# Row maxima of the second and third pair of units as 64-row pairs, in slots 2 to 6 and 8 to 12

## The chip, the cores and the metric

One core of a Trainium2 chip. The metric is the time of one execution on the device in microseconds (us), median of the runs.

## The reference

A block of attention over images. x has 4 images of 256 channels and 32 x 32 = 1024 pixels. Cut to what matters:

```
x_n = group_norm(x, 32 groups) * gn_w + gn_b
q, k, v = 1x1 convolutions of x_n (256 x 256 weights and a bias each)
split into 4 heads of 64 channels
attn = softmax(q k^T / 8) over 1024 keys
out = x + 1x1 convolution of (attn v)
```

All is float32.

## The kernel before

**Units and slots.** An image has 8 units; a unit is one head and one half (512) of the queries. In order they are heads 0 and 1 of half 0, heads 0 and 1 of half 1, then heads 2 and 3 likewise. A unit takes 4 slots of 256 keys, so there are 32 slots to an image and 128 in all, G = 0 to 127. A pair V is units 2V and 2V+1: one half of the queries of two heads whose channels share one tile of 128 rows, 64 rows each.

**One slot.** TensorE (PE) forms the scores of 256 keys by 512 queries (`scores`, L711: four matmuls of 512 columns) in one of two double banks of PSUM: st[0] for even slots, st[1] for odd ones. ScalarE (ACT) takes the exponential twice (`exponent`, L909), once to 16 bits (p_hi) and once to 32 bits: into SBUF for odd slots (and slot 0), back into the scores' own bank for even ones. The difference, p_lo, is made by VectorE (DVE) for even slots, one slot later and in two halves (`p_low`, L1023), and by GpSimd (POOL) for the others. Four slots later PE weighs the values (`weigh`, L738: 24 narrow matmuls); after a unit's four slots DVE divides by the sums (`normalise`). Every second slot a job (a convolution of q, k, v or of the output) is begun on PE at its end and finished in the slot after, then evicted by ACT and split into high and low halves by POOL, whose tiles kq_hi and kq_lo hold one tile of 128 channels. SP copies these by DMA into k_both, k_one, q_twice and q_max, which the scores read.

**Maxima.** The softmax needs for each query a shift near its greatest score. PE forms the scores once more with the 16-bit values, 128 queries by 512 keys at a time, DVE reduces them (`row_max`, L995), after a unit's last one makes the shift (`row_shift`, L1010), and SP sends it by DMA as a row into q_max (`shift_to_row`, L490). The first scores of a unit wait for that (L719). A single maximum (L664, `single_maximum`) is one matmul on 128 rows (high and low keys) for one unit, in one of the two mx banks, and a reduction of 512. A pair (L679, `pair_of_maxima`) is two matmuls on 64 rows each, one per head, and a reduction of 2 x 512, in both mx banks or in the scores bank st[1]: there it waits for the odd slot's exponential (L690), and the next scores in st[1] wait until it is read (L728).

**Where they stand.** The order is written out by hand. Units 0 and 1 have singles straight from the tiles of k and q, begun ahead of slot 0 and ended in slot 1. Units 2 and 3 have singles from q_twice and k_both, two a slot: unit 2 in slots 2 to 5, unit 3 in slots 6 to 9. V = 2 (units 4 and 5) has pairs in slots 6, 8, 10, 10, 11, 12, 12, 13 (`FIRST_PAIRS`). V = 3 begins in slot 14, two to every even slot. In an even slot PE issues a pair's matmuls ahead of the weighing, in an odd listed slot behind it.

**Queues.** Each engine runs its own list in order. DVE's slot (in `slot` under `vector`): p_lo of the even slot before, then the maxima and a shift, the statistics of the next image, `normalise`, last single maximum of the slot; in slots 1 and 2 one half of channel_stats ends the slot. POOL's slot: cast and split of a job two slots back, p_lo, then the rest. The cast (`high`, L1219) waits until the tile's readers are done. SP first sends the shifts completed in the slot before, then its copies.

Of the kernel before, what the change touches and what calls it, by code (L numbers as in the profile page):

```python
# [12 lines left out]
def attention_block(nc, x, gn_w, gn_b, wq, bq, wk, bk, wv, bv, wp, bp, out):  # L13
# [9 lines left out]
    QT = HALF // P  # L23
# [6 lines left out]
    LAG = 4  # L30
    MX_AHEAD = 6
    MXJ = 2 * QT
    SINGLES = 4
    PAIR_AHEAD = 10
    PR = 8
    PB = 3
# [34 lines left out]
    FIRST_IMAGE = {0: ("q", 1, 0, 0), 2: ("v", 0, 1, 0), 4: ("k", 1, 1, 0), 6: ("q", 1, 1, 0), 8: ("v", 1, 0, 0)}  # L71

    MAX_MIDWAY = ((), (), ((0, 0), (0, 1)), ((0, 4), (0, 5)), (), ())
    FIRST_PAIRS = {6: (0,), 8: (1,), 10: (2, 3), 11: (4,), 12: (5, 6), 13: (7,)}
    FIRST_IN_SCORES = (0, 1, 2, 5)
    MAX_AFTER = ((), (), ((0, 2), (0, 3)), ((0, 6), (0, 7)), ((1, 0), (1, 1)), ((1, 2), (1, 3)))
    WARM = 4
    TAIL = 5
# [5 lines left out]
    with ctx:  # L84
# [153 lines left out]
        def wait(eng, s, v):  # L238
            if v > 0:
                eng.wait_ge(s, v)  # L240
# [41 lines left out]
        def pair_maxima(G):  # L282

            V, m = divmod(G + PAIR_AHEAD, 2 * SPU)
            if G in FIRST_PAIRS:
                return [("two", SINGLES // 2, m) for m in FIRST_PAIRS[G]]
            if V == LAST_PAIR:
                return [("two", V, m)]
            if m % 2 or not SINGLES // 2 < V < LAST_PAIR:
                return []  # L290
            return [("two", V, m), ("two", V, m + 1)]

        def in_scores_bank(V, m):

            return m in FIRST_IN_SCORES if V == SINGLES // 2 else V < LAST_PAIR and m % 2 == 0

        def maxima_at(G):
            return pair_maxima(G) + single_maxima(G)
# [12 lines left out]

        def one_slot_later(kind, n, m):

            return kind == "two" and SINGLES // 2 < n < LAST_PAIR and m % 2 == 1

        def reduced_at(G):

# [21 lines left out]

        def mx_part(U, j):  # L340

            return (j % QT, j // QT) if U < 2 else (j // 2, j % 2)

        def pair_part(m):
            return m % QT, m // QT

        def joined(U):

            return U + 1 if U < SINGLES else SINGLES + (U - SINGLES) // 2 + 1

        def units_joined(U):

# [13 lines left out]
        def tile_of(half, tile):  # L366

            return slice(half * HALF + tile, (half + 1) * HALF, QT)
# [9 lines left out]
        def unit(U):  # L378

            b, u = divmod(U, UNITS)  # L380
            return b, 2 * (u // 4) + u % 2, (u // 2) % 2
# [210 lines left out]
        def _(pe):  # L592
# [68 lines left out]
                                 start=False, stop=True, skip_group_check=True).then_inc(s_stat, 1)  # L661
                taken.append((s_gmean if kind == "mean" else s_gvar, b + 1))

            def single_maximum(U, j):  # L664
                if U < 2:
                    first_maximum(U, j)
                    return
                _, head, half = unit(U)
                if j == 0 and U == 2:
                    pe.wait_ge(s_first_top, 16 * 2)  # L670
                elif j == 0:
                    wait(pe, s_dup_k, 16 * 6)
                    wait(pe, s_dup_q[1], 16 * 6)
                wait(pe, s_mx_free, banks_read(("one", U, j)))
                tile, part = mx_part(U, j)
                nc.tensor.matmul(mxb[j % 2], q_twice[:, head, tile_of(half, tile)], k_both[:, head, halves(part)],
                                 start=True, stop=True).then_inc(s_mx_full, 1)

            def pair_of_maxima(V, m, G):  # L679

                b, head, half = unit(2 * V)
                tile, part = pair_part(m)
                if half == 0:
                    wait_hi(pe, "q", nth(head // 2, 0, b) + 1)
                    wait_hi(pe, "k", nth(head // 2, part, b) + 1)
                elif m == 0:
                    wait(pe, s_dup_k, 16 * 6 * (V // 2 + 1))
                    wait(pe, s_dup_q[1], 16 * 6 * (V // 2 + 1))
                if in_scores_bank(V, m):
                    wait(pe, s_exp, G)  # L690
                    bank = st[1]
                else:
                    wait(pe, s_mx_free, banks_read(("two", V, m)))
                    bank = mx
                for h in range(2):
                    rows = slice(h * D, (h + 1) * D)
                    if half == 0:
                        queries, keys = kq_hi["q"][rows, tile_of(0, tile)], kq_hi["k"][rows, halves(part)]
                    else:
                        queries = q_twice[rows, head + h, tile_of(1, tile)]  # L700
                        keys = k_both[rows, head + h, halves(part)]
                    last = nc.tensor.matmul(bank[:, h * HALF:(h + 1) * HALF], queries, keys, start=True, stop=True)  # L702
                last.then_inc(s_mx_full, 1)

            def maximum(item, G):
                if item[0] == "one":
                    single_maximum(*item[1:])
                else:
                    pair_of_maxima(*item[1:], G)

            def scores(G):  # L711
                U, s = divmod(G, SPU)
                _, head, half = unit(U)
                q = halves(half)
                if G == 1:
                    pe.wait_ge(s_e32["k"], 3)
                    pe.wait_ge(s_e32["q"], 2)
                if s == 0:
                    wait(pe, s_shift_dma[U % 2], 16 * (U // 2 + 1))  # L719
                if s == 0 and U < 2:  # L720
                    pe.wait_ge(s_first[U], 16 * 6)
                if s == 0 and U >= SINGLES and U % 4 == 0:
                    wait(pe, s_dup_k, 16 * 6 * (U // 4 + 1))
                    wait(pe, s_dup_q[0], 16 * 6 * (U // 4 + 1))
                if G > 1 and not in_place(G - 2):
                    wait(pe, s_exp, G - 1)
                if pair_in_bank(G) is not None:
                    wait(pe, s_mx_free, pair_in_bank(G) + 1)  # L728
                for c in range(CPS):
                    if G > 1 and in_place(G - 2):  # L730
                        wait_p_lo(pe, G - 2, c)
                    k = slice((CPS * s + c) * P, (CPS * s + c + 1) * P)
                    dst = st[G % 2][:, c * HALF:(c + 1) * HALF]
                    nc.tensor.matmul(dst, k_both[:, head, k], q_twice[:, head, q], start=True, stop=False)  # L734
                    last = nc.tensor.matmul(dst, k_one[:, head, k], q_max[:, head, q], start=False, stop=True)  # L735
                last.then_inc(s_st, 1)
# [464 lines left out]
        def _(pool):  # L1201
# [17 lines left out]
            def high(kind, i, j, b):  # L1219
                wait(pool, s_e32[kind], nth(i, j, b) + 1)  # L1220
                wait(pool, s_dup_k if kind == "k" else s_dup_q[j], 16 * 6 * (2 * b + i))
                if (i, b) == (1, 0):
                    wait(pool, s_mx_full, 2 * MXJ)
                elif (i, b) > (0, 0):
                    gone = 2 * (2 * b + i - 1)
                    if kind == "k":
                        wait(pool, s_mx_full, place_of["two", gone, (j + 1) * QT - 1] + 1)
                    elif j == 0:
                        wait(pool, s_mx_full, all_full("two", gone))
                nc.gpsimd.tensor_copy(kq_hi[kind][:, halves(j)], e32[kind][:, j, :]).then_inc(s_hi[kind], 1)  # L1230
# [40 lines left out]
            def slot(G):  # L1271
                b, g = place(G)
                todo = job_at(G - 2) if G % 2 == 0 else None
                if todo and todo[0] in "kq":
                    high(*todo)
                    low_kq(pool, *todo)
                if todo and todo[0] == "v":
                    split_values(*todo[1:])
                if slot_of(G - 1) is not None and not lo_on_dve(G - 1):
                    p_low(G - 1)  # L1280
                if G == 1:
                    high("k", 1, 0, 0)
                    low_kq(pool, "k", 1, 0, 0)
                if todo and todo[0] == "y":
                    residual(*todo[1:])
                if output_at(G):
                    split_output(*output_at(G))
                stat = stat_at(G)
                if G % 2 and job_at(G - 1) and job_at(G - 1)[0] not in LONG:
                    stat = job_at(G - 1)  # L1290
                if stat and stat[0] == "mean":
                    about_group_mean(pool, stat[-1])
                if stat and stat[0] == "var":
                    norm_factors(stat[-1])
                lows = FIRST_Z_LOW if b == 0 else Z_LOW
                if b + 1 < B and g in lows:
                    z_low(pool, b + 1, lows.index(g))
                if b == B - 1 and g in (21, 23):
                    add_bias((g - 21) // 2)
# [52 lines left out]
```

## Time and profile before

| | us |
|---|---|
| median of 3 runs | 366.53 (366.32 to 366.99) |
| the profiled execution | 366.61 |
| its span | 364.9 |
| PE busy | 348.4 (95%) |
| ACT busy | 302.1 (83%) |
| POOL busy | 284.2 (78%) |
| DVE busy | 283.2 (78%) |

TensorE's granted clock is full in all 40 slices of the span. Matmuls overlap: the time of one in a row is from its start to its modelled end, and what it takes of PE is the distance between two starts. PEld is the load of weights, SPq the queue of SP's DMA issues.

### The profile page before, as it was taken

To read this page: it belongs to the slowest core of one execution; us is meant where nothing else is said; L and a number is where in the kernel's file an instruction comes from. 1 tells how busy PE (TensorE), PEld (TensorE's weight loads), DVE (VectorE), ACT (ScalarE), POOL (GpSimd) and SP (SyncE) were. 2 spreads that over 40 slices of the span, in tenths; PEclk is the share of its full clock that TensorE was granted. 3 is DMA by queue.
4 is the path that set the end of the run, shared out by engine and by line. 5 is a ranking of instruction groups with operands and counts; after the bars stand their busy time and mean duration, and the time that the engine had idled before them with its cause. 6 is when DMAs were issued, how large, how long until landed. Compare 5 with 4: busy or idle time off the path is not lost.

```text
span 364.9 us, 11249 instructions
## 1 busy us (share of the span) xinstructions
PE 348.4 (95%) x4581; PEld 209.4 (57%) x4581; DVE 283.2 (78%) x445; ACT 302.1 (83%) x361; POOL 284.2 (78%) x258
## 2 busy tenths in 40 slices
PE   0999999999999999999999999999999999999996
PEld 0634564655656565655666556565656556655564
DVE  4889899878888687878887777777877787787474
ACT  1748879998887999989877999988889888888982
POOL 5064989699778998988778998988979797967722
PEclk9999999999999999999999999999999999999999
DMA  6046241123743440261643342031552451060113
GB/s 206 25 131 160 45 97 38 31 91 85 135 129 74 93 98 31 29 184 38 131 146 66 72 88 70 8 82 43 117 164 50 96 91 60 2 203 2 31 31 118
DMA packets 38731, 30.92 MB, mean 85 GB/s; under 512 B 23820, under 2 KB 31512, under 8 KB 38680
## 3 DMA queue, kind: packets, MB, share of 16 engines
q1 hardware_dynamic: 37936, 29.15, 32.8%
q10 hardware_dynamic: 744, 1.06, 0.8%
q8 instruction: 37, 0.61, 0.7%
q14 instruction: 14, 0.11, 0.1%
HBM read 9.44 MB, written 4.19 MB: 37 GB/s over the span
## 4 chain that ended last, share of the span: by engine, by line
PE 84%; DVE 9%; ACT 2%; issue 2%; DMA 1%; DVEq 1%; POOL 0%; ACTq 0%
PE gen L612 19%; PE st L734 13%; PE st L735 13%; PE pv L757 9%; PE pv L760 8%; PE pv L759 7%; PE st L702 5%; PE mx L702 3%; DVE mx L1003 3%; PE st L612 2%; DVE p_lo L1029 2%; PE mx L815 1%; ACT st L924 1%; DVE mx L999 1%; DMA xin<-in_x_dram 1%
## 5 line engine op out<-in xcount | busy, mean ns | idle before, releaser
L919 ACT ACTIVATE p_hi<-st 128x1024 f16<-128x1024 f32 x127 | 130.7, 1029 | 41.2 <-PE st L735 40.6
L1268 POOL TENSOR_TENSOR p_lo<-p,p_hi 128x1024 f16<-128x1024 f32 x62 | 132.2, 2132 | 10.2 <-ACT p L924 10.2
L757 PEld LDWEIGHTS pv<-v_hi,p_hi 128*128 128x128 f16 x1024 | 93.4, 97 | 26.7 <-issue 14.7
L757 PE MATMUL pv<-v_hi,p_hi 128*128 128x65 f16 x1024 | 106.5, 195 | 0.3 <-DVE o L1037 0.2
L759 PE MATMUL pv<-v_lo,p_hi 128*128 128x64 f16 x1024 | 106.0, 193 | 0.0
L760 PE MATMUL pv<-v_hi,p_lo 128*128 128x65 f16 x1024 | 105.8, 194 | 0.0
L1029 DVE TENSOR_TENSOR p_lo<-st,p_hi 128x512 f16<-128x512 f32 x126 | 80.9, 684 | 31.6 <-ACT st L924 31.3
L734 PE MATMUL st<-q_twice,k_both 128*128 128x512 f16 x256 | 97.1, 379 | 1.6 <-DVE p_lo L1029 1.2
L759 PEld LDWEIGHTS pv<-v_lo,p_hi 128*128 128x128 f16 x1024 | 93.9, 99 | 6.2
L735 PE MATMUL st<-q_max,k_one 65*128 65x512 f16 x256 | 97.3, 380 | 0.0
L760 PEld LDWEIGHTS pv<-v_hi,p_lo 128*128 128x128 f16 x1024 | 93.9, 97 | 0.0
L1003 DVE TENSOR_REDUCE mx<-st 128x2 f32<-128x1024 f32 x52 | 63.7, 1226 | 24.2 <-PE st L702 24.0
L1003 DVE TENSOR_REDUCE mx<-mx 128x2 f32<-128x1024 f32 x60 | 73.1, 1218 | 1.6 <-PE mx L702 1.6
L924 ACT ACTIVATE st<-st 128x1024 f32<-128x1024 f32 x63 | 65.6, 1041 | 0.0
L924 ACT ACTIVATE p<-st 128x1024 f32<-128x1024 f32 x64 | 65.2, 1018 | 0.0
L734 PEld LDWEIGHTS st<-q_twice,k_both 128*128 128x128 f16 x256 | 25.4, 99 | 26.3 <-issue 6.9
L735 PEld LDWEIGHTS st<-q_max,k_one 65*128 65x128 f16 x256 | 25.0, 98 | 18.4
L453 POOL TENSOR_TENSOR st_lo_k<-e_k,st_hi_k 128x512 f16<-128x512 f32 x16 | 18.5, 1157 | 9.6 <-ACT e_k L894 7.6
L1247 POOL TENSOR_TENSOR y<-y,xres 128x512 f32<-128x512 f32 x14 | 17.7, 1269 | 7.6 <-ACT y L903 7.6
L999 DVE TENSOR_REDUCE mx<-mx 128x1 f32<-128x512 f32 x32 | 20.9, 685 | 2.9 <-PE mx L815 1.4
L612 PE MATMUL gen<-w_hi_v,z_hi 128*128 128x128 f16 x128 | 23.1, 219 | 0.0
L612 PE MATMUL gen<-w_hi_v,z_lo 128*128 128x128 f16 x128 | 23.0, 219 | 0.0
(183 smaller groups left out, 545.0 us busy)
## 6 DMA issues: line engine op xcount, KB each, us to landing
q_twice<-st_hi_q SPq DMA_DIRECT2D x64, 64.0 KB, 2.1
xres<-in_x_dram SPq DMA_DIRECT2D x4, 1024.0 KB, 5.2
out_dram<-y SPq DMA_DIRECT2D x13, 256.0 KB, 2.3
xin<-in_x_dram SPq DMA_DIRECT2D x6, 512.0 KB, 4.7
k_both<-st_hi_k SPq DMA_DIRECT2D x16, 128.0 KB, 2.3
k_one<-st_hi_k SPq DMA_DIRECT2D x16, 128.0 KB, 2.6
q_max<-st_lo_q SPq DMA_DIRECT2D x32, 64.0 KB, 2.1
k_both<-st_lo_k SPq DMA_DIRECT2D x16, 128.0 KB, 2.3
```

The lines of the kernel that those rows point to most:

```text
L612: last = nc.tensor.matmul(dst, a, c, start=first and t == 0 and n == 0, stop=t == CT - 1 and n == 2, skip_group_check=True)
L702: last = nc.tensor.matmul(bank[:, h * HALF:(h + 1) * HALF], queries, keys, start=True, stop=True)
L734: nc.tensor.matmul(dst, k_both[:, head, k], q_twice[:, head, q], start=True, stop=False)
L735: last = nc.tensor.matmul(dst, k_one[:, head, k], q_max[:, head, q], start=False, stop=True)
L757: nc.tensor.matmul(pv_v[:, q, :], hi, vh, start=k == 0 and q == 0, stop=False, skip_group_check=True)
L759: nc.tensor.matmul(pv_v[:, q, 0:D], hi, vl, start=False, stop=False, skip_group_check=True)
L760: last = nc.tensor.matmul(pv_v[:, q, :], lo, vh, start=False, stop=k == NK - 1, skip_group_check=True)
L919: nc.scalar.activation(p_hi[:, G % PR, :, :], scores, ACT.Exp, scale=SM_SCALE / M_SCALE)
L924: nc.scalar.activation(p_full(G), scores, ACT.Exp, scale=SM_SCALE / M_SCALE).then_inc(s_exp, 1)
L1003: last = nc.vector.reduce_max(mx8[:, n % 2, :, tile, part], bank[:, :].rearrange("p (h k) -> p h k", h=2), AX.X)
L1029: nc.vector.tensor_tensor(p_lo[:, G % PR, c, :], p_full(G)[:, c, :], p_hi[:, G % PR, c, :], ALU.subtract).then_inc(s_plo_dve, 1)
L1268: nc.gpsimd.tensor_tensor(p_lo[:, G % PR, :, :], p_full(G), p_hi[:, G % PR, :, :], ALU.subtract)\
```

## The change

Units 2 and 3 lose their singles. They become the pairs of V = 1, straight from the tiles of k and q, in slots 2 to 6 (two pairs in even slots, one in odd ones). The pairs of V = 2 go to slots 8 to 12 in the same pattern. In each, pairs 0, 3 and 6 use the scores bank. Both shifts of units 2 and 3 are now made in slot 6. Since V = 1 reads the tile of k, POOL's cast of the second tile of k over its first half goes from slot 1 to slot 5 and waits for pairs of V = 1; the casts after it wait likewise. The first scores of unit 2 get a wait for the copies of q.

```
-    SINGLES = 4
+    SINGLES = 2
+    BY_LIST = 2
...
-    FIRST_PAIRS = {6: (0,), 8: (1,), 10: (2, 3), 11: (4,), 12: (5, 6), 13: (7,)}
-    FIRST_IN_SCORES = (0, 1, 2, 5)
+    FIRST_PAIRS = {2: ((1, 0), (1, 1)), 3: ((1, 2),), 4: ((1, 3), (1, 4)), 5: ((1, 5),), 6: ((1, 6), (1, 7)),
+                   8: ((2, 0), (2, 1)), 9: ((2, 2),), 10: ((2, 3), (2, 4)), 11: ((2, 5),), 12: ((2, 6), (2, 7))}
+    FIRST_IN_SCORES = {1: (0, 3, 6), 2: (0, 3, 6)}
...
             if G in FIRST_PAIRS:
-                return [("two", SINGLES // 2, m) for m in FIRST_PAIRS[G]]
+                return [("two", *pair) for pair in FIRST_PAIRS[G]]
...
-            return m in FIRST_IN_SCORES if V == SINGLES // 2 else V < LAST_PAIR and m % 2 == 0
+            return m in FIRST_IN_SCORES[V] if V <= BY_LIST else V < LAST_PAIR and m % 2 == 0
...
-            return kind == "two" and SINGLES // 2 < n < LAST_PAIR and m % 2 == 1
+            return kind == "two" and BY_LIST < n < LAST_PAIR and m % 2 == 1
...
             def pair_of_maxima(V, m, G):
...
-                if half == 0:
-                    wait_hi(pe, "q", nth(head // 2, 0, b) + 1)
+                if half == 0 or V == 1:
+                    wait_hi(pe, "q", nth(head // 2, half, b) + 1)
...
-                    if half == 0:
-                        queries, keys = kq_hi["q"][rows, tile_of(0, tile)], kq_hi["k"][rows, halves(part)]
+                    if half == 0 or V == 1:
+                        queries, keys = kq_hi["q"][rows, tile_of(half, tile)], kq_hi["k"][rows, halves(part)]
...
             def scores(G):
...
+                if s == 0 and U == 2:
+                    wait(pe, s_dup_q[1], 16 * 6)
...
             def high(kind, i, j, b):
...
                 if (i, b) == (1, 0):
-                    wait(pool, s_mx_full, 2 * MXJ)
+                    if kind == "k":
+                        wait(pool, s_mx_full, place_of["two", 1, (j + 1) * QT - 1] + 1)
+                    else:
+                        wait(pool, s_mx_full, 2 * MXJ if j == 0 else all_full("two", 1))
...
-                if G == 1:
+                if G == 5:
                     high("k", 1, 0, 0)
                     low_kq(pool, "k", 1, 0, 0)
```

`single_maximum` and `joined` are removed, being without a caller.

## Rows read from the trace of the kernel before

**Rows 1.** The page: busy time by engine, and the chain's shares.
```profile
PE 348.4 (95%) x4581; PEld 209.4 (57%) x4581; DVE 283.2 (78%) x445; ACT 302.1 (83%) x361; POOL 284.2 (78%) x258
...
PE 84%; DVE 9%; ACT 2%; issue 2%; DMA 1%; DVEq 1%; POOL 0%; ACTq 0%
```

**Rows 2.** Stages: edges, length, then busy us of PE, PEld, DVE, ACT, POOL; clock; DMA.
```profile
32.27:37.09 4.82, 4.32 (x37) 2.51 (x37) 4.42 (x10) 4.50 (x6) 2.49 (x4) 1.00 0.39 83
37.09:49.06 11.97, 11.96 (x138) 6.87 (x139) 10.21 (x20) 8.92 (x11) 11.32 (x12) 1.00 0.28 61
49.06:70.99 21.93, 20.75 (x296) 13.11 (x295) 20.22 (x30) 19.85 (x25) 17.90 (x21) 1.00 0.24 51
```

**Rows 3.** Timeline of PE, slots 3 to 6: start, duration, operation, [idle before].
```profile
34.52 0.38 PE L734 MATMUL st<-q_twice,k_both 128*128 128x512 f16 x1
...
37.09 0.38 PE L734 MATMUL st<-q_twice,k_both 128*128 128x512 f16 x1 [0.44 <-DVE p_lo L1029]
...
37.60 0.39 PE L734 MATMUL st<-q_twice,k_both 128*128 128x512 f16 x1
...
40.25 0.38 PE L734 MATMUL st<-q_twice,k_both 128*128 128x512 f16 x1
...
42.92 0.38 PE L734 MATMUL st<-q_twice,k_both 128*128 128x512 f16 x1
...
43.58 0.38 PE L735 MATMUL st<-q_max,k_one 65*128 65x512 f16 x1
43.89 0.41 PE L702 MATMUL st<-st_hi_k,st_hi_q 64*128 64x512 f16 x2
44.23 0.41 PE L676 MATMUL mx<-k_both,q_twice 128*128 128x512 f16 x1
```

**Rows 4.** Timeline of DVE, slots 2 to 6.
```profile
34.22 1.29 DVE L999 TENSOR_REDUCE mx<-mx 128x1 f32<-128x512 f32 x2
35.43 0.68 DVE L1058 BATCH_NORM_STATS2 bn<-xin 128x6 f32<-128x512 f32 x1
...
36.31 1.24 DVE L1029 TENSOR_TENSOR p_lo<-st,p_hi 128x512 f16<-128x512 f32 x2
37.46 1.88 DVE L999 TENSOR_REDUCE mx<-mx 128x1 f32<-128x512 f32 x3
...
44.34 1.23 DVE L1003 TENSOR_REDUCE mx<-st 128x2 f32<-128x1024 f32 x1
45.48 0.68 DVE L999 TENSOR_REDUCE mx<-mx 128x1 f32<-128x512 f32 x1
```

**Rows 5.** Timeline of SP's DMA issues: the shift of unit 1.
```profile
34.78 0.51 SPq L494 DMA_DIRECT2D q_max<-shift  x1
```

**Rows 6.** Timeline of PE's weight loads, the first of slot 4.
```profile
37.06 0.10 PEld L734 LDWEIGHTS st<-q_twice,k_both 128*128 128x128 f16 x1 [0.73 <-DMA q_max<-shift]
```

**Rows 7.** The tile shift, whole kernel: its 32 DMAs.
```profile
DMA to landing us min/median/max: 1.9/2.0/3.5
```

**Rows 8.** Timeline of ACT, the two exponentials of slot 5.
```profile
41.32 1.02 ACT L919 ACTIVATE p_hi<-st 128x1024 f16<-128x1024 f32 x1 [1.13 <-PE st L735]
42.24 1.02 ACT L924 ACTIVATE p<-st 128x1024 f32<-128x1024 f32 x1
```

**Rows 9.** Timeline of PE, slot 16: weighing begins behind two pairs.
```profile
72.51 0.20 PE L757 MATMUL pv<-v_hi,p_hi 128*128 128x65 f16 x1
```

**Rows 10.** Timeline of DVE, slot 13: last maximum of V = 2 and its shift.
```profile
65.10 1.23 DVE L1003 TENSOR_REDUCE mx<-mx 128x2 f32<-128x1024 f32 x1
...
66.75 0.17 DVE L1020 TENSOR_SCALAR shift<-mx 128x8 f16<-128x8 f32 x1
```

**Rows 11.** Timeline of POOL: casts of k in slots 1 and 6, z_b.
```profile
34.69 0.61 POOL L1230 CAST st_hi_k<-e_k 128x512 f16<-128x512 f32 x1 [2.19 <-SPq L578]
...
45.17 0.61 POOL L1230 CAST st_hi_k<-e_k 128x512 f16<-128x512 f32 x1
...
52.40 0.20 POOL L1217 TENSOR_TENSOR z_b<-beta_z,z_m 128x2 f32<-128x2 f32 x1
```

More of the change, by code:

```diff
@@ L285, in pair_maxima @@
             if G in FIRST_PAIRS:
-                return [("two", SINGLES // 2, m) for m in FIRST_PAIRS[G]]
+                return [("two", *pair) for pair in FIRST_PAIRS[G]]
             if V == LAST_PAIR:
                 return [("two", V, m)]
-            if m % 2 or not SINGLES // 2 < V < LAST_PAIR:
+            if m % 2 or not BY_LIST < V < LAST_PAIR:
                 return []
@@ L340, in mx_part @@
         def mx_part(U, j):
-            return (j % QT, j // QT) if U < 2 else (j // 2, j % 2)
+            return j % QT, j // QT
         def pair_part(m):
             return m % QT, m // QT
-        def joined(U):
-            return U + 1 if U < SINGLES else SINGLES + (U - SINGLES) // 2 + 1
         def units_joined(U):
@@ L662, in statistic @@
                 taken.append((s_gmean if kind == "mean" else s_gvar, b + 1))
[L664 to L677, printed above, removed]
             def pair_of_maxima(V, m, G):
@@ L706, in maximum @@
                 if item[0] == "one":
-                    single_maximum(*item[1:])
+                    first_maximum(*item[1:])
                 else:
```

## The prediction

> **What bounds the kernel now.** The page first: PE is busy 95% of the span and holds 84% of the chain that ended last, VectorE (DVE) 9% [rows 1]. So time is gained or lost where PE stands still or gets fewer passes. The change touches slots 1 to 13 only, so the stage table comes next. Its edges are starts of scores: of slot 2 (32.27), 4 (37.09), 8 (49.06) and 16 (70.99). In slots 2 and 3 PE is busy 4.32 of 4.82 us, and DVE, at 4.42, more than PE. In slots 4 to 7 PE is full, 11.96 of 11.97. In slots 8 to 15 it idles 1.18 of 21.93, with DVE busy 20.22 [rows 2]. Two engines are near full at once: work moved forward in DVE's order can stop PE even if there is less of it.
>
> The timeline then shows the links. Scores of an even slot wait for p_lo of the slot two before, which DVE makes in two halves: DVE begins it at 36.31, PE begins the halves of slot 4 at 37.09 and 37.60, so 0.78 and 1.29 later [rows 3, 4]. Those scores also stood behind the DMA of the shift row: issued 34.78, PE's weight load released at 37.06, 2.28 us [rows 5, 6]; over the kernel such DMAs land in 1.9 to 3.5 us [rows 7]. Of the exponential: scores begin at 40.25, ScalarE (ACT) at 41.32 (1.07 later), and its second pass ends at 42.24+1.02 = 43.26, 1.94 after its start [rows 3, 8].
>
> **Prices.** A 512-column pass is 0.22 us of PE: three spacings from 42.92 to 43.58; scores are four, 0.87. A pair between full-height work: scores of slot 6 end at 42.92+0.87 = 43.79, the next operation starts at 44.23, so 0.44 though both halves run at once [rows 3]. Two pairs in a row: 70.99+0.87 = 71.86 to weighing at 72.51, 0.65 [rows 2, 9]. On DVE two single maxima take 34.22 to 35.43 (1.21 to the next operation). One pair's starts 0.45 after its matmuls (43.89, 44.34) and takes 1.23, 1.14 until the next operation (45.48) [rows 3, 4]. The two halves of p_lo take 1.15 to 1.20 (36.31 to 37.46 here; 1.20 is taken). From a unit's last pair maximum to its shift: 65.10+1.23 = 66.33 to 66.75+0.17 = 66.92, 0.59 [rows 10].
>
> Here row and rule can be weighed. By the rows a lone pair (0.44) costs what two singles cost (2 x 0.22); only the second of two pairs is cheap (0.21). The Trainium skill, TensorEngine Tiling (Array Packing), Theoretical Speedup, promises up to 2x at 64 rows or fewer, by which 16 passes would become 8 and PE would save 1.74 us; its Key Properties say that a change of tiling mode drains TensorE, and the trace's 0.44 agrees with that. The sum goes by the rows.
>
> **Step 1, slots 2 to 4: +1.07.** DVE reaches the first maximum of slot 2 at 34.22, behind the shift of unit 1 and channel_stats, as now [rows 4]. There stand two singles (1.21); the change puts two pairs there (2.28), both ahead of the other half of channel_stats and p_lo of slot 2. p_lo goes from 36.31 to 37.38. Two things follow. The first pair is in the scores bank, so scores of slot 3, now at 34.52, wait until it is read: 34.22+1.23 = 35.45, about +1.0. Scores of slot 4 wait for p_lo: 38.16 and 38.67 for 37.09 and 37.60, +1.07.
>
> **Step 2, slot 4: +0.52.** Scores end at 39.1, the first pair runs to 39.44, and the second needs the maxima bank: DVE starts slot 3's pair only after p_lo, 37.38+1.20 = 38.58, and ends at 39.81. Second pair from 39.9 to 40.24. What is left of the 2.65 from the late half to the next scores (37.60 to 40.25) without that half (0.44), two singles (0.44) and some 0.16 of waiting is 1.6 for weighing, statistic and job: next scores at about 41.84, against 40.25, +1.59 in all. All of PE's queue stands behind this wait: the weighing, the mean's matmul, the job whose tile POOL splits. Low end +0.07 (the wait hidden), high +0.6.
>
> **Step 3, slots 5 to 7: -0.42.** Slot 5 swaps two singles for a lone pair (0.43, 0.44): nothing. Slot 6 saves 0.22 of passes, but its second pair waits for slot 5's, issued last thing in that slot: nothing again. Slot 7 loses two singles, -0.43; PE could begin scores of slot 8 at 49.06+1.07+0.52-0.42 = 50.23.
>
> **Step 4, slot 8: +0.97.** The lead shrinks: unit 2's shift, now made in slot 5, comes with unit 3's at the end of slot 6. Scores of slot 6 start at 42.92+1.59 = 44.51; slot 5's pair just before at 44.17, reduced to 45.85; the two of slot 6 follow on DVE from 45.93: 1.14+1.23 = 48.30, shift 48.89, DMA issued at 48.92, landed 2.28 later: 51.20. PE waits 0.97. With the landing at 1.9 or 3.5 us it is 0.59 or 2.19. Queued behind: slot 8's scores, both pairs, a weighing and the job. The wait added there for q's copies costs nothing: SP issues them ahead of unit 1's shift (34.78), so they land some 13 us earlier.
>
> **Step 5, slots 8 to 15: -0.65.** Before: five lots of pairs (three lone, two double) and four singles: 3x0.44+2x0.65+4x0.22 = 3.50; after, three doubles and two lone: 2.83. DVE has 4 x 0.60 less and the same pairs, but these stand closer: in slots 10 to 14 three doubles, the p_lo passes, normalise and the shift follow one another. I take PE's saving alone; bounds 0 (DVE keeps the pace) and -1.2 (all 1.18 of idle time goes too). Unit 4's shift comes one slot sooner, and does not bound now.
>
> **Moved on other queues: 0.** On POOL the cast of k (0.61) and its split leave slot 1, where it idled 2.19 us behind SP's count, for slot 5 [rows 11]. q's then stands first at the same count, and the time saved is handed back in slot 5. There the wait on the fourth pair (PE at 39.2) is over; slot 6's cast of k, now at 45.17, waits for the eighth (46.4), with a split, p_lo and the norm factors behind it. z_b, now ready at 52.60, moves as far, to 53.8; ACT asks for it after slot 8's exponential, at 51.20+1.07+1.94 = 54.2. If that cover goes, the excess falls on ACT. SP issues the same shift DMAs, two together instead of one and one; its copies of k wait for that split and are not read before slot 16. From slot 16 the order is the old one and PE the limit, so the lag stays.
>
> **The sum.** +1.07+0.52-0.42+0.97-0.65 = +1.49. The profiled execution took 366.61 us (span 364.9 and 1.7 around it), so 368.1 on its own time; it lies 0.08 above the median 366.53, so **368.0** on the median. Bounds: all low ends 1.07+0.07-0.42+0.59-1.20 = +0.1; all high ends 1.07+0.6-0.42+2.19+0 = +3.4.
>
> **Rivals.** *PE's passes decide, faster.* If DVE's early maxima were off the path, only the passes would count: slots 2 to 7 hold twelve singles and a lone pair, 3.08, and get 2.83: -0.25; with step 5 -0.9, so 365.6. For: PE full in slots 4 to 7. Against: DVE busier than PE in slots 2 and 3. It decides if slot 3's scores start by about 34.7. By the page's 2x this rival would come to 364.8. Chance 0.14.
> *Caught up, no change.* The lag arises but slots 8 to 15 give it back, DVE being freed of 2.4 us of singles and PE having 1.18 of idle there: 1.49-1.2+0.65 less a prompt landing (0.38) is +0.6, and with step 2's wait hidden +0.1: 366.6. For: DVE's 20.22 of 21.93. Against: the pairs crowd in slots 8 to 12. 0.16.
> *The shift lands late.* At 3.5 us, behind other copies, step 4 is 2.19: +2.7, 369.2. For: the largest landing in the view; against: nothing else is issued just ahead. 0.12.
> That the pairs don't run at once is excluded by the row at 43.89.
>
> **How the numbers follow.** Forecast 0.58, so slower (by over 0.2%, 0.73 us, about what a measurement of this kernel can tell from no change) 0.58+0.12 = 0.70; same 0.16; faster 0.14. The range leaves out the faster case and the tail of the late landing: 366.4 to 369.3. The forecast's own range is 367.3 to 368.8.
>
> **What would show it.** Right: slot 3's scores wait for a DVE maximum until about 35.5; slot 4's start near 38.2; PE stands before slot 8's scores for the shift's DMA, about 1 us; from slot 16 on scores stand 1.5 us later than before, constant to the end. Wrong: scores of slot 8 by 49.5, or a lag that shrinks to nothing by slot 16.

## The result, and the profile after

The changed kernel takes 369.14 us (median; 368.69 to 370.04) against 366.76 for the kernel before: ratio 1.0067, 95% interval 1.0053 to 1.0081, so 2.4 us slower. The forecast was slower by 1.5 (368.0), the range 366.4 to 369.3. The profiled execution took 370.04 us (span 368.3), the longest of its four.

The page after, its lines of busy time and of the chain's shares, to set beside [rows 1]:

```profile
PE 348.7 (95%) x4581; PEld 209.6 (57%) x4581; DVE 282.4 (77%) x435; ACT 302.4 (82%) x361; POOL 284.0 (77%) x258
...
PE 83%; DVE 8%; ACT 3%; issue 2%; DVEq 2%; DMA 2%; ACTq 0%
```

No engine works more than 0.3 us longer; the other 3 of the 3.4 us that the span grew are waiting. The stages, as in [rows 2], at the starts of scores of slots 2, 4, 8 and 16:

```profile
34.04:39.94 5.90, 4.62 (x40) 2.47 (x40) 5.50 (x10) 4.53 (x6) 4.21 (x4) 1.00 0.40 90
39.94:52.53 12.59, 11.80 (x138) 6.52 (x138) 10.61 (x17) 9.08 (x11) 10.11 (x12) 1.00 0.06 11
52.53:73.82 21.29, 20.15 (x293) 12.59 (x293) 17.39 (x23) 19.79 (x25) 17.55 (x20) 1.00 0.33 71
```

The lengths were 4.82, 11.97 and 21.93: slots 2 and 3 gained 1.08, slots 4 to 7 gained 0.62, slots 8 to 15 lost 0.64. That is 1.06 in all, and the same steps can be followed slot by slot. Below, a lag is the start of a slot's first exponential less that of slot 2, minus the same difference in the trace of the kernel before. ACT's rows for slots 2 and 16, before:

```profile
33.35 1.02 ACT L919 ACTIVATE p_hi<-st 128x1024 f16<-128x1024 f32 x1
...
72.61 1.04 ACT L919 ACTIVATE p_hi<-st 128x1024 f16<-128x1024 f32 x1
```

and after, where the difference is 40.32 instead of 39.26:

```profile
35.13 1.03 ACT L904 ACTIVATE p_hi<-st 128x1024 f16<-128x1024 f32 x1
...
75.45 1.04 ACT L904 ACTIVATE p_hi<-st 128x1024 f16<-128x1024 f32 x1
```

From there the lag is constant: 1.06 at slot 16, 1.11 at slot 126. Two more parts lie outside the changed slots. Slot 2's exponential is already 1.78 later than before, and from slot 126's exponential (352.72 before, 355.61 after) to the end of the span it takes 12.69 us instead of 12.18. The sum is 1.78+1.11+0.51 = 3.40.

DVE in slots 2 to 4 after, to set beside [rows 4]:

```profile
36.00 1.23 DVE L988 TENSOR_REDUCE mx<-st 128x2 f32<-128x1024 f32 x1
37.14 1.22 DVE L988 TENSOR_REDUCE mx<-mx 128x2 f32<-128x1024 f32 x1
38.27 0.68 DVE L1043 BATCH_NORM_STATS2 bn<-xin 128x6 f32<-128x512 f32 x1
39.02 0.21 DVE L1045 BATCH_NORM_AGGREGATE mv<-bn 128x2 f32<-128x12 f32 x1
39.15 1.23 DVE L1014 TENSOR_TENSOR p_lo<-st,p_hi 128x512 f16<-128x512 f32 x2
40.30 1.22 DVE L988 TENSOR_REDUCE mx<-mx 128x2 f32<-128x1024 f32 x1
```

and PE's rows that waited for it, then the first scores of slot 8 (beside [rows 3]):

```profile
37.37 0.38 PE L719 MATMUL st<-q_twice,k_both 128*128 128x512 f16 x1 [0.71 <-DVE mx L988]
...
39.94 0.38 PE L719 MATMUL st<-q_twice,k_both 128*128 128x512 f16 x1 [0.52 <-DVE p_lo L1014]
...
41.66 0.41 PE L685 MATMUL mx<-st_hi_k,st_hi_q 64*128 64x512 f16 x2 [0.27 <-DVE mx L988]
...
52.53 0.39 PE L719 MATMUL st<-q_twice,k_both 128*128 128x512 f16 x1 [0.42 <-DMA q_max<-shift]
```

Each predicted wait is there: slot 3's scores for the first pair, slot 4's for p_lo, the second pair of slot 4 for the bank, slot 8's for the shift. The last is shorter than reckoned: SP issued that DMA at 50.59 and PE went on 1.94 us later, not 2.28.

```profile
50.59 1.15 SPq L492 DMA_DIRECT2D q_max<-shift  x2
```

What was not predicted stands ahead of slot 2. PE's eight warming passes take 1.91 us, the first pass of the first job 0.63 instead of 0.39 (the granted clock reads 1.00 in this stretch in both traces), and the first scores wait 1.13 us for the first shift row, whose DMA landed in 3.5 us instead of 1.9:

```profile
13.08 1.91 PE L814 MATMUL st<-group_avg,ident 128*128 128x128 f32 x8
14.78 0.63 PE L610 MATMUL st<-z_hi,w_hi_q 128*128 128x512 f16 x1
...
29.19 0.38 PE L719 MATMUL st<-q_twice,k_both 128*128 128x512 f16 x1 [1.13 <-issue]
```

The same passes in the trace of before:

```profile
13.16 1.12 PE L829 MATMUL st<-group_avg,ident 128*128 128x128 f32 x8
14.38 0.39 PE L612 MATMUL st<-z_hi,w_hi_q 128*128 128x512 f16 x1
```

### The profile page after: what moved, and what is told of

It reads as the page before. It is cut to its first block, busy times and chain, and to the rows that moved or that the text cites. A ratio compares the mean times of both kernels' runs of the same rounds, so it can differ in the third digit from the quotient of the medians.

```text
span 368.3 us, 11245 instructions
## 1 busy us (share of the span) xinstructions
PE 348.7 (95%) x4581; PEld 209.6 (57%) x4581; DVE 282.4 (77%) x435; ACT 302.4 (82%) x361; POOL 284.0 (77%) x258
## 3 DMA queue, kind: packets, MB, share of 16 engines
q10 hardware_dynamic: 744, 1.06, 0.8%
HBM read 9.44 MB, written 4.19 MB: 37 GB/s over the span
## 4 chain that ended last, share of the span: by engine, by line
PE 83%; DVE 8%; ACT 3%; issue 2%; DVEq 2%; DMA 2%; ACTq 0%
PE gen L610 19%; PE st L719 13%; PE st L720 13%; PE pv L742 9%; PE pv L745 7%; PE pv L744 7%; PE st L685 5%; PE mx L685 4%; DVE mx L988 4%; DVE p_lo L1014 2%; PE st L610 2%; DVEq L978 2%; ACT st L909 1%; PE mx L800 1%; DMA xin<-in_x_dram 1%
## 5 line engine op out<-in xcount | busy, mean ns | idle before, releaser
L988 DVE TENSOR_REDUCE mx<-st 128x2 f32<-128x1024 f32 x54 | 66.2, 1226 | 26.5 <-PE st L685 26.3
L988 DVE TENSOR_REDUCE mx<-mx 128x2 f32<-128x1024 f32 x66 | 80.4, 1218 | 3.8 <-PE mx L685 3.8
L610 PE MATMUL gen<-w_lo_v,z_hi 128*128 128x128 f16 x128 | 23.0, 219 | 0.0
```

The lines of the kernel that those rows point to most:

```text
L610: last = nc.tensor.matmul(dst, a, c, start=first and t == 0 and n == 0, stop=t == CT - 1 and n == 2, skip_group_check=True)
L988: last = nc.vector.reduce_max(mx8[:, n % 2, :, tile, part], bank[:, :].rearrange("p (h k) -> p h k", h=2), AX.X)
```

## The experiments

Theory: the slots lose 1.06 us by DVE's order and the shift's lead, the rest is start and end. Rivals: PE's passes or the exponentials hold the slots, or the start belongs to the changed program. The lags, with ratios to the kernel before measured beside each run:

| run | lag at slot 3 | 5 | 8 | 16 | ratio (interval) |
|---|---|---|---|---|---|
| changed kernel | 1.07 | 1.58 | 1.70 | 1.06 | 1.0067 (1.0053 to 1.0081) |
| changed, again | 1.07 | 1.58 | 1.70 | 1.06 | 1.0050 (1.0031 to 1.0069) |
| statistics later | 1.07 | 0.76 | 0.88 | 0.23 | 1.0036 (1.0016 to 1.0056) |
| earlier seventh pair | 1.07 | 1.58 | 1.58 | 0.77 | 1.0019 (1.0000 to 1.0038) |
| 16 memsets | 1.07 | 1.58 | 1.70 | 1.05 | 1.0035 (1.0020 to 1.0049) |
| V = 2 spread | 1.07 | 1.58 | 1.70 | 1.32 | 1.0055 (1.0042 to 1.0068) |
| later half and seventh pair | 1.07 | 0.77 | 1.52 | 0.72 | 1.0037 (1.0023 to 1.0051) |
| both halves and seventh pair | 0.57 | 0.27 | 1.02 | 0.21 | 1.0035 (1.0020 to 1.0051) |
| both halves, memsets | 0.58 | 0.28 | 0.39 | -0.25 | 0.9990 (0.9975 to 1.0006) |
| the same, odd pairs ahead | 0.58 | 0.28 | 0.57 | -0.13 | 0.9993 (0.9980 to 1.0006) |

**Both kernels again**, without an edit. The kernel before:

> The kernel before, unchanged, once more. In the changed kernel's trace the first exponential starts at 30.26 us against 28.36, ahead of every slot that the change touches: 0.7 us of TensorE at a lower granted clock and a first shift row that landed in 3.5 us instead of 1.9. Theory A (chance of the execution): the start varies from run to run, so this trace may show the first exponential anywhere from 28.4 to 30.3, and the ratio is 1.000 within 0.002. Theory B (the changed program's own start): here the first exponential stays near 28.4 and the shift lands in about 2 us.

The lower granted clock of which this expectation speaks does not stand ahead of slot 2 in the changed kernel's trace: it reads 1.00 in every stretch up to 367 us, and 0.50 only in the last 1.3 us, when PE has no work left.

Ratio 0.9996 (0.9979 to 1.0013). Its profiled execution was a long one (369.58): the first shift landed in 3.4 us, the first exponential started at 29.64, and a granted clock of 0.51, near the lower of its two levels, between 30.3 and 33.7 us (0.78 over 28 to 32) took slot 2 to 36.07. So a late first landing and a disturbed start belong to the execution. The lags stay: -0.11 at slot 8 and -0.12 at slot 16.

> The changed kernel, unchanged, once more. Theory A: the first exponential comes back towards 28.4 us and the time towards the kernel before plus the slots' own 1.1 us, a ratio of about 1.003. Theory B: the first shift row lands in 3.5 us again, the first exponential starts near 29.5, and the ratio stays at 1.006 to 1.007. Both: from slot 2 to slot 15 the exponentials fall back by 1.06 us against the kernel before.

The lags are those of the first trace. The landing was 1.9 us here, yet the ratio is 1.0050 and the first exponential started at 29.07, 0.71 late: neither theory holds whole. Of the 2.3 us that its span (367.2) is longer, 0.71 lie ahead of slot 2, 1.02 are the lag at slot 126 and 0.57 come behind it.

**The second half of the statistics later:**

```diff
-                if G in (1, 2):
-                    channel_stats(1, 1, (G - 1,))
+                if G in (1, 3):
+                    channel_stats(1, 1, (G // 2,))
```

> The changed kernel with the second half of channel_stats moved from the end of DVE's slot 2 to the end of its slot 3, so that p_lo of slot 2 follows the two pairs directly. My theory of step 1 (DVE's work ahead of p_lo holds PE): scores of slot 4 start 0.6 us sooner after those of slot 2 and those of slot 5 0.85 sooner than in the changed kernel, and the whole is 0.8 us faster than it. Rival (the exponential or the passes of PE hold slots 3 and 4): no change against the changed kernel.

Lag at slot 5 0.76 instead of 1.58, at slot 16 0.23 instead of 1.06: 0.83 gained, against 0.8 expected. DVE's rows of slots 2 and 3 show p_lo directly behind the pairs:

```profile
34.62 1.23 DVE L988 TENSOR_REDUCE mx<-st 128x2 f32<-128x1024 f32 x1
35.77 1.22 DVE L988 TENSOR_REDUCE mx<-mx 128x2 f32<-128x1024 f32 x1
36.90 1.28 DVE L1014 TENSOR_TENSOR p_lo<-st,p_hi 128x512 f16<-128x512 f32 x2
38.09 1.22 DVE L988 TENSOR_REDUCE mx<-mx 128x2 f32<-128x1024 f32 x1
39.23 0.68 DVE L1043 BATCH_NORM_STATS2 bn<-xin 128x6 f32<-128x512 f32 x1
```

Scores of slot 4 start 0.60 us sooner after those of slot 2, and those of slot 5 0.82 sooner. No pass of PE and no exponential changed, so from slot 4 on it is DVE's order that holds PE, and the rival falls. Slot 3's lag is still 1.07: this edit leaves what stands ahead of the first pair as it was. In times the gain does not stand clear: the median is 368.43 against 368.96 for the changed kernel beside it, and the two ratios' intervals overlap.

**The seventh pair of V = 1 in slot 5:**

```diff
-... 5: ((1, 5),), 6: ((1, 6), (1, 7)),
+... 5: ((1, 5), (1, 6)), 6: ((1, 7),),
-    FIRST_IN_SCORES = {1: (0, 3, 6), 2: (0, 3, 6)}
+    FIRST_IN_SCORES = {1: (0, 3, 7), 2: (0, 3, 6)}
         def ahead_of_weighing(G):
...
+            if G == 5:
+                return 1
```

> The changed kernel with the seventh pair of V = 1 moved from slot 6 to slot 5 (the sixth ahead of the job and the weighing there, the seventh behind them), so that slot 6 has one pair and the shift is ready about 0.45 us sooner after the first scores of slot 5 and PE's wait for its DMA before slot 8 (0.42 us in the changed kernel's trace) is gone. My theory of step 4: slot 8's scores start 0.4 us sooner against those of slot 2 than in the changed kernel, the whole 0.4 us faster than it. Rival (the passes alone count): within 0.1 us of it.

The wait for the DMA ahead of slot 8 is gone, but slot 5 is 0.45 longer (lag at slot 6 2.05 instead of 1.60), so slot 8's lag fell by 0.12 only, not 0.4; at slot 16 by 0.29. The last pair, now in the scores bank, also made slot 7's scores wait 0.21 for the shift itself. The direction was right, the gain smaller.

**Sixteen memsets.** DVE lost ten instructions by the change. The DMA view of the changed kernel's trace between 365.4 and 366.4 us, 2.75 us ahead of the end, has

```profile
q14 instruction: 1, 0.01, 4.6%
```

In the first trace of the kernel before the last packet of that queue is 7.25 us ahead of the end. (A packet of the other instruction queue, q8, is 4.5 us ahead of the end there, and 7.0 in the changed kernel.) The four last DVE operations of the changed kernel take

```profile
363.81 1.56 DVE L1055 SCALAR_TENSOR_TENSOR y<-st,xres 128x256 f32<-128x256 f32 x4 [0.68 <-PE st L610]
```

where they take 1.42 before. That is 0.14 of the 0.51 us; the other 0.38 lie between the last of them and the end (2.93 us against 2.55), where only output DMAs are left. The edit:

```diff
+        spare = sb("spare", [P, 16])
...
+                if 36 <= G < 52:
+                    nc.vector.memset(spare[:, G - 36:G - 35], 0.0)
```

> The changed kernel plus 16 one-element memsets on DVE into a tile that nothing reads, one in each of slots 36 to 51. The four traces of changed programs have a packet of the instruction queue 14 about 2.8 us ahead of the end, the two of the kernel before at 7.3; from the 127th exponential to the end of the span they take 12.7 to 13.0 us against 12.2 and 12.5. Theory (fewer DVE instructions move a fetch of code into the last output): here the packet is no longer in the last 4 us, that stretch takes 12.2 to 12.5 and the kernel is 0.4 us faster than the changed one, with the same lag of 1.06 us from slot 2 to 15. Rival (the stretch is long for another reason): 12.7 and the same time.

Nothing useful was added, and the end came back: the packet is 8.25 us ahead, the stretch behind slot 126's exponential 12.20 us, the four operations

```profile
362.97 1.42 DVE L1056 SCALAR_TENSOR_TENSOR y<-st,xres 128x256 f32<-128x256 f32 x4 [0.69 <-PE st L611]
```

The lag did not move. The ratio is 1.0035 here, 1.0050 and 1.0067 without, and the intervals of the first two overlap; its own trace had a late first landing (3.5 us) again. Over all traces the stretch is 12.16 to 12.20 us in the three programs with the memsets, 12.69 to 12.97 in the seven traces without, and 12.11 to 12.49 in four of the kernel before. So the packet's place moves with the number of DVE instructions (435, 445 and 451), and the longer end goes with it. That this packet itself holds up the last output is argued, not shown.

**V = 2 spread:**

```diff
-... 8: ((2, 0), (2, 1)), 9: ((2, 2),), 10: ((2, 3), (2, 4)), 11: ((2, 5),), 12: ((2, 6), (2, 7))}
+... 8: ((2, 0),), 9: ((2, 1),), 10: ((2, 2), (2, 3)), 11: ((2, 4),), 12: ((2, 5), (2, 6)), 13: ((2, 7),)}
-    FIRST_IN_SCORES = {1: (0, 3, 6), 2: (0, 3, 6)}
+    FIRST_IN_SCORES = {1: (0, 3, 6), 2: (0, 2, 5)}
```

> The changed kernel with the pairs of V = 2 over slots 8 to 13 in the numbers 1, 1, 2, 1, 2, 1, as the kernel before has them over 6 to 13, instead of 2, 1, 2, 1, 2. Step 5 by PE's passes: two doubles and four lone pairs in place of three and two cost 0.23 us, so the lag at slot 16 is 1.3 instead of 1.06. Rival (DVE's crowd in slots 10 to 14 bounds): the lag at slot 16 is 0.8 or less.

1.32 at slot 16, from 1.06, as expected, but not for the reason expected. From one slot's first scores to the next, slot 8 is 0.15 us shorter here than in the changed kernel (one pair instead of two), slot 13 is 0.20 shorter although it has a pair more, and slot 14 is 0.62 longer. There the second pair of V = 3 waits for the maxima bank, since the last maximum of V = 2 is made in slot 13 again and its shift comes that much later. The kernel before has the same row,

```profile
66.98 0.41 PE L702 MATMUL mx<-k_both,q_twice 64*128 64x512 f16 x2 [0.45 <-DVE shift L1020]
```

and the changed kernel has no such wait; there scores of slot 14 wait for p_lo instead:

```profile
68.45 0.39 PE L719 MATMUL st<-q_twice,k_both 128*128 128x512 f16 x1 [0.48 <-DVE p_lo L1014]
```

This part of the change is worth its 0.26 us, by waits more than by the price of passes.

**Later half and seventh pair together** (the second and third diff):

> The later half of channel_stats and the earlier seventh pair together, on the changed kernel. If steps 1 and 4 are two separate waits on one path, the savings add up: 0.83 and 0.29 of the lag of 1.06 at slot 16, leaving -0.1 to 0.0 against the kernel before. If one hides the other: +0.2 as with the statistics alone. The median is then 0.3 to 1 us above the kernel before, from the start and the last microseconds.

Wrong: 0.72 at slot 16, worse than the statistics alone. The trace shows where the gain went, in slot 5, for which the sixth pair has to be read first:

```profile
45.32 0.41 PE L687 MATMUL mx<-st_hi_k,st_hi_q 64*128 64x512 f16 x2 [0.51 <-DVE mx L990]
```

PE is 0.8 us earlier, but DVE begins to reduce the sixth pair 9.84 us after slot 2's exponential, against 9.89 with the seventh pair moved alone: the statistics moved to slot 3 stand ahead of it on DVE. So PE now waits for DVE there. The savings are on one path and don't add.

**The first half moved, too**, between the single maxima of slot 1:

```diff
+                if G == 1:
+                    channel_stats(1, 1, (0,))
                 for item in tops[early:]:
...
-                if G in (1, 3):
-                    channel_stats(1, 1, (G // 2,))
+                if G == 3:
+                    channel_stats(1, 1, (1,))
```

> As the one with both, and the first half of channel_stats moved up between the two single maxima of slot 1, into DVE's idle time there, so that the first pair of slot 2 is reduced some 0.4 us sooner. If DVE's queue ahead of that pair is what holds slot 3 (step 1), the third exponential's lag falls from 1.07 to about 0.7, and the lag at slot 16 to -0.3 to -0.5. If the pair's own matmuls or the exponential hold it: 1.07 and no more gain.

Slot 3's lag fell to 0.57, further than the 0.7 expected, so DVE's queue ahead of the first pair makes about half of that lag; at slot 16 it is 0.21, not -0.3 to -0.5, because the seventh pair's wait in slot 5 (lag from 0.27 to 1.48 at slot 6) was still in it. Without that edit, and with the memsets:

> The changed kernel with both halves of channel_stats out of the way of the first pairs (the first between the two single maxima of slot 1, the second at the end of slot 3), the seventh pair back in slot 6, and the 16 memsets. From the runs so far: lag at slot 16 with the second half moved +0.22, less the 0.5 that the first half gave at slot 3, is -0.3 against the kernel before; the last 12 us as in the padded kernel. Theory: DVE's queue ahead of p_lo was the whole of steps 1 and 2, so this is level with the kernel before or up to 0.3 us under it, ratio 0.999 to 1.001 (1.002 if the start is slower). Rival: some other wait takes over and the lag stays above +0.2.

-0.25 at slot 16, ratio 0.9990 (0.9975 to 1.0006): level with the kernel before, as expected. A lag of 0.58 at slot 3 and 0.28 at slot 5 remains, which later slots give back. The kernel before was not run with the statistics moved, so this does not tell what the same move is worth there. **The lone pairs ahead of the weighing:**

```diff
-            return 0 if G in FIRST_PAIRS and G % 2 else len(pairs)
+            return len(pairs)
```

> The same, and the lone pairs of odd slots issued ahead of the weighing instead of behind it. The waits of the second pairs of slots 6 and 10 for the bank (0.27 and 0.26 us in the changed kernel's trace) should go: lag at slot 16 some 0.2 to 0.5 lower than without, -0.5 to -0.8. Rival: the wait for the shift's DMA ahead of slot 8 grows by what PE gains, and DVE bounds slots 10 to 14: no change at slot 16.

The rival was right: what PE gains it waits for the shift. Slot 6's second pair now starts 0.24 us behind the first instead of 0.50, so its wait for the bank is gone, but the shift is issued at 47.53 us against 47.57. At slot 16 the lag is 0.12 higher, about as much as traces of one kernel differ. The first scores of slot 8 without this edit,

```profile
49.50 0.39 PE L720 MATMUL st<-q_twice,k_both 128*128 128x512 f16 x1 [0.41 <-DMA q_max<-shift]
```

and with it:

```profile
49.47 0.39 PE L720 MATMUL st<-q_twice,k_both 128*128 128x512 f16 x1 [0.71 <-DMA q_max<-shift]
```

**The start of the kernel before, twice more:**

> The kernel before, for the start alone. In its two traces PE's eight warming passes ahead of the first job take 1.06 and 1.12 us, in the eight traces of changed programs 1.39 to 1.92. If that is the chance of the execution, traces of the kernel before should show 1.4 or more too; if it is the program's own, about 1.1 again.

> As the third: 1.4 us or more for the eight warming passes if the start is chance, about 1.1 if it is the program's own.

The warming passes took 1.06 and 1.20 us; one of the rows:

```profile
12.94 1.06 PE L829 MATMUL st<-group_avg,ident 128*128 128x128 f32 x8
```

Four traces of the kernel before have 1.06 to 1.20, ten of changed programs 1.39 to 1.92. That speaks for the program, but no edit was found that governs it, and not every long row costs: with both halves moved it is 1.46, and the first exponential starts at 28.41. The cause stays open.

These passes are only one part of a late start. DVE's first statistics wait for x, and begin at 4.33 to 4.74 us in the four traces of the kernel before and at 4.19 to 4.95 in the ten of changed programs, so that part varies in both. From there to the first shift on DVE it is 20.13 to 20.14 us in the kernel before; in changed programs it is 20.14 where the passes take 1.39 us, 20.46 where they take 1.70 and 21.05 where they take 1.92. Of the 0.71 us by which the changed kernel's second trace starts late, 0.39 are x and 0.32 these passes.

The single times were 366.25 and 366.46 us. Their lags at slot 16 (-0.10 and -0.11) agree with the -0.12 of the first repeat: the trace that all lags are taken against is the odd one, 0.11 us longer in slot 6. Against the other three every lag from slot 7 on would be 0.11 higher, 1.17 at slot 16 for the changed kernel.

## Why the prediction was right, and where it was off

**What bounds.** Right: the loss is waits of PE behind DVE's order in slots 2 and 3 and for the shift row at slot 8; the lag is constant from slot 16 on.

**Step 1**, +1.07: measured 1.07. **Step 2**, +0.52: 0.52 (1.58 less 1.06). That DVE's order makes them is shown by moving statistics: the later half took 0.82 of the 1.58 at slot 5 back, both halves 0.50 of the 1.07 at slot 3 and 1.30 at slot 5.

**Step 3**, -0.42: the lag at slot 8 is 1.70 with 0.42 of waiting in it, so without the wait 1.28; from 1.58 that is -0.30, of which 0.11 belong to the long slot 6 of the reference trace.

**Step 4**, +0.97, is the term that was mis-sized: 0.42. The step took 2.28 us from issue to release from the one case of [rows 5, 6], while 2.0 was the median of [rows 7], and in the changed kernel PE went on after 1.94. The 2.28 was no landing time: for that very DMA (33 to 36 us of the trace before) the view of the tile shift has

```profile
DMA to landing us min/median/max: 1.9/1.9/1.9
```

so the weight load of [rows 6] was held some 0.4 us beyond the landing; the matmul beside it waited for p_lo [rows 3]. Of the 0.55 too much, 0.34 are this; the rest is an issue 0.10 sooner and a PE 0.11 later than reckoned. With 0.59, the low end given for it, the sum would have been 1.11, against a lag of 1.06.

**Step 5**, -0.65 (its own prices give -0.67): 1.70 to 1.06 is -0.64, and the agreement is in part luck. The step let PE's passes alone count: 0.23 less in slot 8, 0.44 less in slot 13. Slot 8 did shrink by 0.23 (3.18 to 2.95). Slot 13 lost its pair and yet grew by 0.21 (2.02 to 2.23), since scores of slot 14 then waited 0.48 for p_lo. Slot 14 shrank by 0.62 (3.73 to 3.11), since its second pair no longer waited 0.45 for the bank. The step reckoned with neither wait, and the two nearly made up for each other. The spread pairs, +0.26 against 0.23, came out right in the same way.

**Other queues**, nothing: nearly. ACT waited 0.23 us for z_b, which came at 55.76 against 52.60. The prediction thought it ready in time; in the kernel before ACT already waited 0.56 for it, so this wait became shorter, and it cost nothing.

**The sum.** The slots cost 1.06, less than the 1.49 foretold, and the kernel lost 2.4. What failed is the tacit step that nothing outside the changed slots moves. The end took 0.5 more, together with an instruction-queue packet that ten DVE instructions fewer moved into it; the memsets undid both. The start took 0.4 to 0.8 more in five of the eight traces of changed programs with a prompt first landing: in part x's arrival, which varies in both kernels, in part the warming passes, cause open. These errors had opposite signs to step 4's, and it was luck that the range held the result, by 0.16 us.

**The rivals.** PE's passes alone (faster) is excluded by the waits at slots 3 and 4. Caught up: slots 8 to 15 gave back 0.64, not more. A late landing did not happen at slot 8 in any trace, but did for the first shift in three, the kernel before's among them.

The rows' price of pairs stood the test in two slots. Slot 9 swaps two singles for a lone pair and is 2.70 us before and 2.71 after; slot 8 swaps a lone pair and two singles for two pairs and gains 0.23. The Trainium skill, TensorEngine Tiling (Array Packing), Theoretical Speedup, gives up to 2x for short rows. A lone pair gained none of it here. Its Key Properties name a drain at a change of mode; the 0.44 of a lone pair against the 0.21 of a second one would fit that, but no run tests it apart.

## What to carry to other kernels

Ask of work that is moved forward not how long it takes but what stands behind it in its engine's queue: two maxima instead of two shorter ones cost 1.07 us because p_lo, on which PE waits, was next. Two savings on one path seldom add, so measure them together. When a small change alters the time by more than the trace of its own slots explains, compare the first and last microseconds of both programs: here ten instructions fewer on one engine went with an end 0.5 us longer. And check a term that came out right slot by slot: two waits left out of step 5 made up for each other.

## What the runs showed of the hardware

A packet of an instruction queue 2.75 us ahead of the end went with an end 0.5 us longer; 16 one-element memsets 300 us earlier moved it to 8.25 us and the stretch from 12.69 to 12.20 us. The same 1 KB DMA of the first shift row landed in 1.9 to 2.3 us in most traces and in 3.4 or 3.5 in three, of both kernels; a late one shifts the whole execution by 1.1 to 1.2 us.
